# A GpSimd memset of 288 columns behind every gather of a graph-network kernel

## What is computed

```python
# layer 0
msg = relu((x[src] * edge_weight[:, None]) @ W_msg + b_msg)
agg = segment_sum(msg, dst)
x1  = layernorm(x + relu(agg @ W_out + b_out))
# layers 1 and 2 (weights w1, sl1, b1, then w2, sl2, b2), h = x1 at first
xt  = einsum('nd,rde->rne', h, W)      # 8 products for each node
h   = relu(segment_sum(xt[edge_type, src], dst) + h @ SW + b)
out = layernorm(x1 + h)
```

## Time and profile before

| | us |
|---|---|
| median of the three timed runs | 6096.66 |
| the profiled execution, span from first to last instruction | 7175.4 |
| GpSimd busy in it | 4562.2 |
| VectorE busy | 2671.7 |
| TensorE busy (matmul) | 2668.5 |
| ScalarE busy | 606.3 |

### The profile page before, as it was taken

The page is one execution under the profiler, slowest core; times in us unless marked ns, Lnnn a source line. Parts: engine busy times, 40 slices in busy tenths (PEclk is TensorE's granted clock), DMA queues, the critical chain, the costliest instruction groups (busy, mean ns, idle before and its releaser), DMA issues.

```text
span 7175.4 us, 45352 instructions
## 1 busy us (share of the span) xinstructions
PE 2668.5 (37%) x11892; PEld 2091.2 (29%) x11892; DVE 2671.7 (37%) x5892; ACT 606.3 (8%) x1334; POOL 4562.2 (64%) x4835
## 2 busy tenths in 40 slices
PE   4334344433444343444444444443223223222223
PEld 4333333322333322223332333332222222222222
DVE  3776666666555532333332222232111111111112
ACT  2111111111111110000000000000000000000000
POOL 4666666666666646666666666665666666666665
PEclk9666666666666656666666666665555555555556
DMA  5122222222222212222222222221111111111111
GB/s 144 43 78 74 71 73 72 73 74 71 73 74 72 74 55 61 70 68 70 69 69 69 68 67 67 69 70 57 52 52 52 52 53 51 52 52 51 52 51 49
DMA packets 265749, 468.98 MB, mean 65 GB/s; under 512 B 102461, under 2 KB 155365, under 8 KB 265477
## 3 DMA queue, kind: packets, MB, share of 16 engines
q0 software_dynamic: 154112, 315.93, 17.0%
q1 hardware_dynamic: 110212, 149.64, 6.1%
q10 hardware_dynamic: 1152, 0.39, 0.0%
HBM read 343.56 MB, written 122.05 MB: 65 GB/s over the span
## 4 chain that ended last, share of the span: by engine, by line
another core or an unknown queue 48%; DVE 22%; issue 17%; PE 10%; DVEq 2%; ACT 1%; DMA 0%; SPq 0%; POOL 0%; ACTq 0%; POOLq 0%
PE bank L791 6%; DVE rows L769 5%; PE bank L1031 3%; DVE picked L1070 2%; DVE work L751 2%; DVE place L1081 2%; DVE onehot L751 2%; DVE tab L1091 1%; DVEq L776 1%; DVE agg L781 1%; DVE bank L1385 1%; DVE work L1386 1%; DVE bank L1383 1%; DVE work L1390 1%
## 5 line engine op out<-in xcount | busy, mean ns | idle before, releaser
L688 POOL DMA_INDIRECT rows<-rel_table,rel_index x3152 | 2980.9, 946 | 1643.4 <-issue 939.0
L688 POOL DMA_INDIRECT rows<-msg_table,msg_index x1600 | 1514.0, 946 | 918.9 <-issue 466.9
L791 PE MATMUL bank<-work,rows 128*128 128x128 f32 x6304 | 1188.1, 336 | 1300.7 <-issue 1282.2
L781 DVE TENSOR_TENSOR agg<-agg,bank 128x128 f32 x602 | 171.2, 284 | 3803.2 <-remote 3486.7
L791 PEld LDWEIGHTS bank<-work,rows 128*128 128x128 f32 x6304 | 1084.7, 249 | 1438.0 <-issue 1419.9
L791 PE MATMUL bank<-onehot,rows 128*128 128x128 f32 x3328 | 624.5, 361 | 890.6 <-ACT rows L657 498.8
L791 PEld LDWEIGHTS bank<-onehot,rows 128*128 128x128 f32 x3328 | 583.4, 268 | 960.3 <-ACT rows L657 524.1
L1031 PE MATMUL bank<-wr,feat 128*128 128x512 f32 x784 | 598.5, 907 | 693.1 <-issue 429.7
L751 DVE TENSOR_TENSOR work<-bank,place 128x1024 f32<-128x1024 f32 x394 | 477.1, 1212 | 7.3 <-ACT agg L956 3.8
L1031 PEld LDWEIGHTS bank<-wr,feat 128*128 128x128 f32 x784 | 207.2, 293 | 898.8 <-issue 619.6
L1020 PE MATMUL bank<-ident,sums 128*128 128x128 f32 x98 | 38.1, 389 | 1055.3 <-ACT sums L994 842.8
(11 more groups left out here) (126 smaller groups left out, 1437.0 us busy)
## 6 DMA issues: line engine op xcount, KB each, us to landing
rel_table<-tab SPq DMA_DIRECT2D x196, 512.0 KB
rows<-rel_table,rel_index POOLq DMA_INDIRECT x3152
rows<-msg_table,msg_index POOLq DMA_INDIRECT x1600
x_dram<-normed SPq DMA_DIRECT2D x98, 64.0 KB
xin<-x_dram SPq DMA_DIRECT2D x98, 64.0 KB
xin<-in_x_dram SPq DMA_DIRECT2D x97, 64.0 KB
out_dram<-normed SPq DMA_DIRECT2D x97, 64.0 KB
tab<-in_x_dram SPq DMA_DIRECT2D x24, 256.0 KB
```

The costliest lines, as they stand in the source:

```text
L688: nc.gpsimd.indirect_dma_start(rows[:, u, t, :], None, table, bass.IndirectOffsetOnAxis(ap=table_index[:, g, t:t + 1], axis=0)).then_inc(e ...
L781: nc.vector.tensor_tensor(out=window, in0=window, in1=sum_of(layer, st), op=ALU.add).then_inc(sems.added, 1)
L791: ins = nc.tensor.matmul(total, tile, hot[:, t, :], start=t == 0, stop=t == TPG - 1)
```

## The change

A buffer `idle` of 128 x 288 float32 is allocated in SBUF. Behind each indirect DMA of `static_gather`, GpSimd fills it with zeros. Each memset waits for the one before it (semaphore `s_rest`), since both write the same buffer. Nobody reads the buffer.

```diff
+        idle = sb("idle", [P, 2 * D + D // 4])
...
+        s_rest = sem("s_rest")
...
+        rests = [0]
+
+        def pool_rest():
+
+            need(nc.gpsimd, s_rest, rests[0])
+            nc.gpsimd.memset(idle[:, :], 0.0).then_inc(s_rest, 1)
+            rests[0] += 1
+
         def static_gather(layer, g):
...
                 ).then_inc(edge_main.rows[u][t // HALF], 16)
+                pool_rest()
```

## The result

The changed kernel takes 7148.45 us (median of four runs, 7147.8 to 7150.22), beside it the kernel before 6097.38 us (four runs, 6094.32 to 6100.25). The ratio is 1.1725 [1.1708, 1.1742]: **1051 us or 17% slower**, 0.218 us for each of the 4816 memsets. The forecast was 7399 us with a range from 7150 us, so the result lies 1.5 us under the range.

What follows compares the result with a forecast made beforehand. The prediction took GpSimd's issue of gathers to bound the kernel end to end. It added 4752 memsets of 0.274 us, 1302 us, to 6096.7 us for 7399 us, 21% slower, with a range of 7150 to 7850 us (chance 0.80).

Steps and rivals of the forecast that it cites:

- GpSimd's issue bounds, end to end: Whole kernel: 4816 gathers, one started every 1.25 us, make 6020 us of the timed 6096.66 us.
- 0.274 us on the path: Behind each gather: a 288-column memset adds 0.274 us start to start; 4752 of them add 1302 us.
- The argument that the gap is the same at group borders: Between gathers: the 0.30 us is equal within and between groups, so held to be GpSimd's own work, not idle.
- The first 64 are covered: Early gathers: 64 memsets, 17.5 us, fit in GpSimd's 62.7 us wait for the message table.
- I take it that the slot waits belong to the profiled execution: GpSimd's ring-slot waits, 986 us in the profile, are taken as absent from the timed runs.
- Rival C: Ring slots hold the timed run too: 12.2 us a group against 11.4, 446 us more, 6543 us; strong form 0.04.
- the 40 us of room in the timed runs: Timed runs leave 77 us beside the gathers, head and tail take 37, so at most some 40 us of waits.
- Rival A: Between gathers: the memset vanishes in the 0.30 us gap, gathers stay 1.25 us apart, 6097 us; chance 0.07.
- B: Between gathers: each change of operation costs extra, 0.364 us and 7826 us, or 8853 us; 0.08 for over 0.37 us.
- D: In `static_gather`: the memsets do not run, since the other path has none; chance below 0.01.
- A port lock by VectorE: L1103 holds the port shared with GpSimd: at most 196 x 0.35 = 68 us, 7467 us; chance 0.05.
- The forecast of the profile: Changed kernel's profile: memset records 0.33 us, gathers 946 ns and 1.52 us apart, slot waits nearly gone, span 7513 us.

Runs made afterwards that it cites:

- the first comparison: Changed kernel (288-column memset behind each gather) against the kernel before, the latter timed without a profile: 7148.45 us beside 6097.38, ratio 1.1725.
- the medians on chip 1: The changed kernel unaltered, run again beside the kernel before on the same chip: 7183.06 us beside 7166.24, ratio 1.0025.

## Why the prediction was wrong, and where it was right

**"GpSimd's issue bounds, end to end": right for the first comparison.**'s spacing accounts for the timed 6097 us, and nearly the whole of what the memsets add to the spacing came out in the time (1045 of 1051 us).

**"0.274 us on the path": this term was mis-sized.** Measured is 0.217 us. The prediction weighed two readings of the 0.30 us between gathers, a hole or GpSimd's own work, and took the second whole. The measured spacing says some 0.055 us of it is free for a following memset, whatever its length: 128 columns cost 0.083 instead of 0.14 us, 192 cost 0.140 instead of 0.194, 264 cost 0.201 instead of 0.254, 288 cost 0.217 instead of 0.274, one column nothing. The term is 4816 x 0.057 = 275 us too large. Its parts, start-to-start and 0.84 ns a column, were right. The argument that the gap is the same at group borders was sound only against the sequencer as its cause; it did not show that none of it could take in a memset. The range reached down to 0.222 us a memset for another reason (GpSimd faster without records); that is not what happened, as the pace of 1.2515 us in the timed runs is the recorded one.

**"The first 64 are covered": not as counted.** The message table's 62.7 us wait was part of the held state, and the changed kernel's is 0.6 us. Without cover 64 x 0.217 = 14 us are added, and the sum is 6097 + 4816 x 0.217 = 7142 us, 6 us under the result. How much was covered in the timed runs is not shown: in the changed kernel's trace TensorE reports the first ring slot free at 96.4 us, and at 1.251 us a gather GpSimd would be there at 90.1 us, so up to 6 of the 14 us may have been.

**"I take it that the slot waits belong to the profiled execution": right in its use, open in its words.** For the time that was asked, the first comparison's, the step held. Whether recording makes the waits is not settled: every execution of the kernel before on the three chips is slow, and every one was recorded. Only their times without a recording would tell it from the chip. The reason that the prediction gave, TensorE's single matmuls 2.1 to 2.8 us apart, is not needed for the hold: with half of the matmuls it stays, and there they run in one go. Rival C priced exactly this, 12.2 us a group against the 11.4 us of the held state; with the true 11.74 us little is left. From 11.85, 11.48 and 11.44 us a group in layers 0, 1 and 2 it is -0.1 x 200 + 0.26 x 197 + 0.30 x 197 = +90 us, and the waits for the three tables end some 49 us (message table) and 59 us (73.3 + 34.4 less 49.1) sooner: -17 us between the two profiles by this sum, -29 us by their spans, and +17 us measured between the medians on chip 1. Its chance of 0.04 rested on the 40 us of room in the timed runs, sound for those and for no others.

**Rival A** (the memset vanishes in the gap) is true in small: 0.057 of 0.274 us. **B** fell, since the price is under 0.274 us. **D**: 4816 memsets ran. A port lock by VectorE was not seen on GpSimd: no gather from `rel_table` took over 967 ns, and 7 of the 4816 memsets took over 0.42 us, 1.8 us more in all. It is VectorE's instruction that grew longer,'s L1103, here L1114 (ns, min/median/max):

```profile
L1114 DVE TENSOR_SCALAR normed<-y,mv,rstd x196: 345/722/843, 253.2 to 7142.8; 128x128 f32<-128x128 f32 x196
```

Its median is 722 ns instead of 347, off the path. The prediction had only the other direction; why it grew was not tested.

**The forecast of the profile**: memset records 0.35 us (forecast 0.33), gathers unchanged at 0.95 us, slot waits gone, span 7146 us instead of 7513 us, since the spacing is 1.468 and not 1.524 us (266 us of it) and since the head and the table waits are shorter.

## What to carry to other kernels

Price filler on a bound engine by the spacing of starts in a pair with its real neighbour: a neighbour's gap can take in a fixed part (here 0.055 us), and a wait on the instruction directly before adds a part of its own (here 0.12 us). Where the profiled execution and the timed runs differ by 17%, time the kernel before again, with and without a recording, on the same chip and on another, before the waits in its profile are called an artefact or real: here a slowdown of 17% in one comparison was one of 0.25% in the other, and the missing pair of times leaves the reason open.

## What had not been expected of the hardware

- An indirect gather's cost on GpSimd is nearly all fixed: 128 rows of 512 bytes 1.251 us, 64 rows 1.208 us, 256 bytes a row 1.251 us.
- In recorded executions on three chips, more than eight gathers in some 11.5 us go with a late semaphore of TensorE, by 19.1 us in the median of layer 2, and the kernel runs at 11.4 us a group. The border is sharp: 240 columns (a gather every 1.431 us, chip 8) are still held a little, 264 (1.452 us, chip 1) are not. Gathers 1.249 us apart within a group are not held where a group takes 13.3 us. The number and the data of the edge matmuls, SyncE's DMAs, GpSimd's one-column memsets, the rows and the bytes of a gather don't move it.
- **Open**: what delays the word of TensorE. In the earlier trace rows its matmuls are recorded 2.1 to 2.8 us apart, but with half of them left out they end in one go and the release is late all the same, so their pace is not needed for the hold. That the gathers' number is what counts is what is left of the things varied (with the number of their packets, which no run separates from it); no run shows the mechanism. Open too is why the first comparison's runs of the kernel before were free of it: they were not recorded, and their chip may be another. The untried run is the kernel before, timed without a recording on chip 8, 1 or 11.
